# A second buffer for the ternarized weights, and one temporary less, in an attention-plus-FFN kernel

## What is computed

```python
x = x + _layernorm(_L0_attn_ref(_layernorm(x), ...))
x = x + _layernorm(_L0_ffn_ref(_layernorm(x), w1, w2))

# attn: u = x @ W_in.T + b_in;  h = lam * h + gamma * u  (scan over the rows);
#       out = h @ W_out.T + b_out + x
def _quant_weight(w):
    s = jnp.clip(jnp.mean(jnp.abs(w)), EPS, None)
    return jnp.clip(jnp.round(w / s), -1.0, 1.0) * s
# ffn: h = gelu(quant_act(x) @ quant_weight(w1).T); quant_act(h) @ quant_weight(w2).T
# w1: 4096 x 1024, w2: 1024 x 4096
```

## Time and profile before

| | us |
|---|---|
| median of two runs | 4675.93 (4628.41 and 4723.45) |
| profiled execution | 4625.51 |
| its span, slowest core (6) | 4624.0 |
| spans of the eight cores | 4595.0 to 4624.0 |
| busy, core 6: PE / DVE / ACT | 2797.7 / 2941.2 / 1673.8 |
| phase A, from the first x block to B1 | about 70 to 1642 |

### The profile page before, as it was taken

The page is one execution under the profiler, slowest core; times in us unless marked ns, Lnnn a source line. Parts: engine busy times, 40 slices in busy tenths (PEclk is TensorE's granted clock), DMA queues, the critical chain, the costliest instruction groups (busy, mean ns, idle before and its releaser), DMA issues.

```text
span 4624.0 us, 40391 instructions; the slowest of 8 cores (4595.0 to 4624.0 us)
## 1 busy us (share of the span) xinstructions
PE 2797.7 (61%) x11916; PEld 1553.3 (34%) x12080; DVE 2941.2 (64%) x2628; ACT 1673.8 (36%) x2053; POOL 201.5 (4%) x372
## 2 busy tenths in 40 slices
PE   5556554444466635455544554455545279999998
PEld 4445443333355512222222222222222134444444
DVE  4767765566677748788877887788878512222232
ACT  1333322222244435555555455545555211111111
POOL 0000000000000000000000000000000000000000
PEclk8766766666677767777777777777777689999999
DMA  3332344455521131212122112211221366666665
GB/s 128 116 103 100 119 128 134 106 130 139 146 73 55 46 109 55 64 62 62 52 64 64 62 50 64 64 62 51 63 64 62 104 121 155 152 151 154 151 154 128
DMA packets 537185, 447.33 MB, mean 97 GB/s; under 512 B 473206, under 2 KB 473208, under 8 KB 524424
## 3 DMA queue, kind: packets, MB, share of 16 engines
q1 hardware_dynamic: 479624, 184.58, 18.0%
q0 software_dynamic: 57344, 260.15, 16.8%
HBM read 193.02 MB, written 151.00 MB: 74 GB/s over the span
## 4 chain that ended last, share of the span: by engine, by line
PE 41%; DVE 13%; DMA 5%; another core or an unknown queue 2%; issue 2%; ACT 1%; DVEq 0%; ACTq 0%; SPq 0%; POOL 0%; POOLq 0%
PE ps_h L911 22%; PE ps_f L1023 19%; DVE amh L148 6%; DMA qdT<-qd 4%; DVE bd L148 3%; DVE cd L148 2%; DVE qd L148 2%; ACT h_b L148 1%; DMA r2B<-r2scr 1%; DVE irc L148 0%; DVEq L135 0%; DVE sch_all L148 0%; DVE bn L148 0%; DVEq L832 0%
## 5 line engine op out<-in xcount | busy, mean ns | idle before, releaser
L911 PE MATMUL ps_h<-w1T,qdT 128*128 128x512 bf16 x4014 | 1025.6, 419 | 982.8 <-DMA qdT<-qd 976.8
L911 PEld LDWEIGHTS ps_h<-w1T,qdT 128*128 128x128 bf16 x4096 | 429.0, 106 | 1579.4 <-issue 1191.7
L1023 PE MATMUL ps_f<-w2T,qhT 128*128 128x512 bf16 x4014 | 881.3, 379 | 95.0 <-DMA qhT<-qhscr 90.6
L148 ACT ACTIVATE h_b<-ps_h,zerov,g3s 128x512 f32<-128x512 f32 x512 | 397.9, 777 | 569.6 <-PE ps_h L911 569.6
L1023 PEld LDWEIGHTS ps_f<-w2T,qhT 128*128 128x128 bf16 x4096 | 401.1, 98 | 575.3 <-issue 93.2
L735 PE MATMUL ps_u<-lnT,winT 128*128 128x256 f32 x2048 | 390.3, 371 | 226.4 <-ACT gu L148 187.8
L148 DVE BATCH_NORM_STATS2 bn<-ffn 128x6 f32<-128x512 f32 x128 | 88.9, 694 | 596.8 <-ACT ffn L148 590.2
L735 PEld LDWEIGHTS ps_u<-lnT,winT 128*128 128x128 f32 x2048 | 376.5, 281 | 246.2 <-issue 243.5
L148 DVE TENSOR_TENSOR bh<-y0h,r16h 128x4096 bf16<-128x4096 f32 x64 | 283.2, 4425 | 209.4 <-ACT r16h L148 209.4
L148 ACT ACTIVATE y0h<-h_b,halfv,sch_all 128x4096 f32<-128x4096 f32 x64 | 243.2, 3801 | 358.4 <-DVE sch_all L148 358.4
L723 PE MATMUL ps_t<-identt,ln1f 128*128 128x128 f32 x512 | 113.6, 395 | 424.8 <-ACT ln1f L148 299.7
(11 more groups left out here) (99 smaller groups left out, 2408.2 us busy)
## 6 DMA issues: line engine op xcount, KB each, us to landing
qstg<-w SPq DMA_DIRECT2D x64, 1024.0 KB, 5.7
qhscr<-qh_b POOLq DMA_DIRECT2D x64, 1024.0 KB, 5.1
x_buf<-x POOLq DMA_DIRECT2D x32, 1024.0 KB, 6.5
r2scr<-r2b POOLq DMA_DIRECT2D x64, 512.0 KB, 2.9
r2B<-r2scr POOLq DMA_DIRECT2D x64, 512.0 KB, 5.8
r2C<-r2scr POOLq DMA_DIRECT2D x64, 512.0 KB, 5.7
y<-outb POOLq DMA_DIRECT2D x64, 512.0 KB, 3.4
w1tscr<-wtp SPq DMA_DIRECT2D x32, 256.0 KB, 2.7
```

Source lines behind the costliest of these rows:

```text
L148: ins = f(*a, **k)
L911: last = t.matmul(ps_h[q % 6][:], qdTv[ta % 2][:, j, :], w1v[:, j, 512 * hs:512 * (hs + 1)], start=(j == 0), stop=(j == DT - 1))
L1023: last = t.matmul(pslice, qhTv[ta % 2][:, j, :], w2v[:, j, 512 * half:512 * (half + 1)], start=(j == 0), stop=(j == HT - 1))
```

## The change

`t2b` becomes two buffers, used in turn; ternarization c2 waits for the pieces of c2-2 instead of c2-1; SP reads the buffer of c2. `tmp1` is removed, and its place is taken by `t2buf` of the same tile, which is no longer needed once `r2b` is made. ACT's wait ahead of `t2buf` goes from `s_r2v` to the semaphore `s_rs2`, which the maximum now raises. Loads, pieces, their order on SP and the division into slots stay.

```diff
-            tmp1 = sbA("tmp1", [128, D], F32)
             qstg = [sbA(f"qstg{i}", [128, 2048], F32) for i in range(2)]
             t1b = sbA("t1b", [128, 2048], BF16)
-            t2b = sbA("t2b", [128, 2048], BF16)
+            t2b = [sbA(f"t2b{i}", [128, 2048], BF16) for i in range(2)]
@@ tern
-                            if c2 >= 1:
+                            if c2 >= 2:
                                 v.wait_ge(sem("s0_xb"),
-                                          16 * pieces_through(c2 - 1))
+                                          16 * pieces_through(c2 - 2))
                             it = v.scalar_tensor_tensor(
-                                t2b[:], qstg[q % 2][:], nthrv[w][:], t1b[:],
-                                op0=ALU.is_le, op1=ALU.subtract)
+                                t2b[c2 % 2][:], qstg[q % 2][:], nthrv[w][:],
+                                t1b[:], op0=ALU.is_le, op1=ALU.subtract)
@@ r2p
-                        v.tensor_scalar(tmp1[:], r2b[ta % 2][:], bn2r[ta % 2][:, 0:1],
+                        v.tensor_scalar(t2buf[ta % 2][:], r2b[ta % 2][:],
+                                        bn2r[ta % 2][:, 0:1],
                                         None, op0=ALU.subtract)
-                        v.tensor_reduce(am3s[:, ta:ta + 1], tmp1[:], axis=AX.X,
-                                        op=ALU.max, apply_absolute_value=True)
+                        iam = v.tensor_reduce(am3s[:, ta:ta + 1], t2buf[ta % 2][:],
+                                              axis=AX.X,
+                                              op=ALU.max, apply_absolute_value=True)
+                        inc("s_rs2", iam)
@@ ln2p (ACT)
                         if ta >= 2:
-                            a.wait_ge(sem("s_r2v"), ta - 1)
+                            a.wait_ge(sem("s_rs2"), ta - 1)
@@ emit_pieces (SP)
-                            xin = t2b[:]
+                            xin = t2b[c2 % 2][:]
-                            xin = t2b[:, 1024 * j:1024 * (j + 1)]
+                            xin = t2b[c2 % 2][:, 1024 * j:1024 * (j + 1)]
```

## The result

| | before | after |
|---|---|---|
| median of all runs, us | 4641.9 (10 runs) | 4504.6 (13 runs) |
| ratio, 95% interval | | 0.9721 (0.9695 to 0.9747) |
| profiled execution, us | 4625.5 | 4493.8 |
| span of the slowest core | 4624.0 (core 6) | 4492.3 (core 3) |
| mean span of the eight cores | 4608.7 | 4482.5 |

The kernel is 2.8% faster. I had said 4504 us, 2.6%. The medians contain executions in which one die ran at a lower clock; the ratio is made without them.

What follows compares the result with a forecast made beforehand. DVE was taken to set phase A's pace, with the `t2b` waits (172.3 us, 21 times) on its path. The terms were 121.55 us and zeros: 4625.5 - 121.6 = 4503.9 us, range 4480 to 4550.

Steps and rivals of the forecast that it cites:

- (a) The buffers: Slots of blocks 12 to 22: each full slot loses one start-to-start time of `t2b`, 121.55 us over eleven windows.
- The third ternarization's load: Slots' third `qstg` load: hidden ahead of the transposes by 3.3 us (w1) or 0.8 us (w2); taken as nothing, bound 37 us.
- (b) SP: SP's queue: later sets still finish before the next slot, even with slot 14's partial sums (48 to 54 against 55); cost nothing.
- threshold of 17 us a set: SP's queue: with three sets a block and the new 51 us period, SP sets the pace from 17 us a set.
- (c) PE's cover: Second matmul section, 10 us: the shorter slot (16.5 us w1, 15 us w2) still covers it; cost nothing, bound 11 us.
- The price of a missing cover: Blocks without a slot: 37.5 us instead of 34.5; for eleven blocks 33 us.
- (d): DVE's subtraction, written to `t2buf` instead of `tmp1`: stays at 0.75 us, cost nothing; 30 us if it ran at 1.23 us.
- (e): ACT's wait ahead of `t2buf`, moved from `s_r2v` to `s_rs2`: nothing new is awaited and nothing comes earlier; cost nothing.
- PE's clock: Rival, `ln1f` transposes: PE's pause falls from 24.55 to about 12 us, its clock stays up, 20 us gained, 4484 us; chance 0.07.
- Nothing gained: Rival, slots: an unseen wait takes the place of the removed one, 4625 us; chance 0.04.
- slower: Rival, SP's queue: SP becomes the bound beside POOL's transfers; at 24.5 us a set 93 us slower, 4718 us; chance 0.04.
- The sum: Whole kernel: 121.55 us saved and zeros, 4625.5 - 121.6 = 4503.9 us; forecast chance 0.74.

Runs made afterwards that it cites:

- the spread kernels: Changed kernel with its 68 tasks spread over all blocks: two a slot, three every eighth block (ratio 0.9533); or three, then two, then one a slot (0.9508).
- the kernel with two stores: Changed kernel in which SP stores every piece twice and waits for each store; ratio to before 0.9962 (0.9927 to 0.9997), mean span 4589.1 us.
- one wait: Changed kernel in which SP stores each piece once and waits for that store; ratio to before 0.976 (0.9706 to 0.9813), mean span 4506.3 us.

## Why the prediction was right, point by point

**(a) The buffers.** Right, and the whole of it: with only the wait undone the gain is 0.0%. The eleven windows said 121.55 us for core 6; the same windows on all eight cores before have a mean of 125.2 us, and the slots gave up 119.0. `t2b` waits 23.9 us in 10, expected about 22 in 10. One reading in it is wrong: slot 16 had not one wait ahead of `t2b` before but two, 13.59 and 9.31 us. The pieces of slot 15's last chunk go out only behind the thresholds, which slot 16 itself computes:

```profile
919.05 2.35 DVE L148 SCALAR_TENSOR_TENSOR t2b<-qstg,nthrv,t1b 128x2048 bf16<-128x2048 f32 x1 [13.59 <-DMA wtp<-t2b]
```

So one of them stays after (3.48 us on core 3). The sum is not touched by this, as what it took for slot 16, 13.05 us from one `t2b` to the next, is the right window.

The missing 6.2 us (125.2 less 119.0) can be placed slot by slot, as the mean length after less the mean length before, less the window: 0.4 us in slot 12, 1.1 and 1.2 in 13 and 14, 2.8 in 15, 0.2 in 16, and nothing in the slots of w2. In w2's slots, where I had seen only 0.8 us between load and transposes, the forecast held to a tenth.

**The third ternarization's load.** I took nothing for it, and the timeline of slot 13 confirms that the load is not what ends last. But it lands later than before, by the median of all loads 6.3 us instead of 5.7. For the load that the third one waits for, in slots 12 to 15, the means of the cores went from 5.4 or 5.5 us to 5.9 to 6.9 us, and the second transpose landed 10.7 to 12.9 us after the load's issue instead of 10.2 or 10.3. So w1's slots take 17 to 18 us and not 16.5. The mechanism was right; the size of one set of w1 was off by about 1 us. The wait of the third `t1b`, forecast as 2 to 3 us, was 2.2 to 3.6 us in the mean of the cores, but 6.7 us in slot 16, beyond the 4 us named as a sign that the load bounds the slot. It doesn't bound it there: `t2b` waits for the transposes behind it all the same. The median:

```profile
DMA to landing us min/median/max: 4.7/6.3/12.9
```

**(b) SP.** Right for all slots but 15, and there in part: it took 16.6 to 24.4 us on the eight cores, 19.6 in the mean. The prediction had SP ready 48 to 54 us after slot 14's start, against a first need at 55. On core 4 the sums were sent and read back so late that the first load went out 5.7 us into the slot instead of 3.8: from the write of the partial sums to their read SP took 17.6 us there, and 12.3 us in the mean of the cores, where the prediction had taken the 11.4 us of core 6. On the other seven it went out on time, but on four of them the transposes behind it took longer. SP's queue on core 0 (21.5 us):

```profile
787.32 0.26 SPq L657 DMA_DIRECT2D qrow<-scrq  x1
789.13 0.39 SPq L679 DMA_DIRECT2D qstg<-w  x1
...
797.36 1.32 SPq L622 DMA_TRANSPOSE wtp<-t2b  x1
804.21 0.51 SPq L632 DMA_DIRECT2D w1tscr<-wtp  x1
```

The second one took until 804.2, 6.9 us where 3.0 is usual, with nothing else of this core on the DMA engines. Why is open; slot 15 costs 2.8 us in the mean. The threshold of 17 us a set that the prediction gave for the rival held: at a mean of 17.8 us slots 12 to 14 grew by about 1 us, at 23.1 us slots 13 and 14 by 16. What the threshold missed is the block with the partial sums, whose room was smaller, and the third set, which stretches more than a lone one.

**(c) PE's cover.** Right: stretches of 381.5 us against 379.6. PE is done with the second product at 706.4, well inside the slot, and its pause is 13.7 us where it was 24.55. Even the products that ran at a mean grant of 0.57 (16.0 us) were covered: behind the slots of blocks 12 to 21 none made DVE wait, neither before (10 of 80) nor after (5 of 80). One of the usual kind:

```profile
704.31 2.12 PE L704 MATMUL ps_a<-woutT,ybf 128*128 128x512 f32 x8
720.11 1.94 PE L725 MATMUL ps_t<-identt,ln1f 128*128 128x128 f32 x8 [13.68 <-ACT ln1f L148]
```

The price of a missing cover, 3.0 us a block, is confirmed by the spread kernels, where blocks 25 to 31 went from 37.5 us to 34.5 us in the mean behind slots of 7.7 us, and to 34.8 us behind slots of mostly 3.85 us.

**(d) and (e).** Right: 0.75 us, and with the `t2buf` edit alone the stretches of blocks 12 to 22 took 380.8 us in the mean of the cores, against 379.7.

**PE's clock.** This rival fell. After the shorter pause the eight transposes of `ln1f` still take 1.94 us, the time at a granted 0.50, and the stretches didn't get shorter. The mean grant of blocks 12 to 22 rose from 0.66 to 0.69 in the mean of the cores. With two levels, 0.5 and 1, that makes 459 us at the low one before (0.34 x 2 x 675) and 341 us after: 118 us less, about what the slots lost. I read this as idle time at the low level that was taken out, while the work runs at the level it had. The Trainium skill ("TensorE: Matmul & The Clock Gate", Part 1) says that the array drops to half rate when it idles; the transposes behind the pause of 13.7 us agree with it.

**Nothing gained, and slower.** Neither came. The Trainium skill ("DMA: Bandwidth & Descriptors", section "Issuing engines are not separate DMA queues") says that DMAs of different issuing engines run on the same 16 DMA engines and interleave. Crowding of this kind has a size now: the third set of w2 took 22.7 us instead of 15.5 in the kernel with two stores. It costs the changed kernel's w2 slots less than 0.1 us each, as it falls into room that exists.

**The sum.** 4503.9 us was expected for an execution like the profiled one, which came out at 4493.8; that the median of all runs is 4504.6 is chance. The sum started from core 6, whose B1 was 19 us longer than the other seven had it, so it was bound to come out high. By the mean spans it reads 4608.7 - 121.6 = 4487.1 us, and 4482.5 was measured: the other cores had more to gain (125.2), the late sets took 6.2 us of it, and stages outside the change happened to be 7 us shorter.

## What to carry to other kernels

When an in-order engine waits in bursts for a serial partner (here DVE for SP's transposes), a second result buffer is worth one partner's turn for each burst, and the start-to-start time of the blocked operation in the trace is that turn, ready to be summed. Before you buy a third buffer, look which wait is next: here the load stood 3 us behind in the slots of w1 and 0.7 us in those of w2. Where side work comes in bursts and part of the blocks have none, spreading it can be worth nearly as much as the buffer (here 1.9% against 2.8%, and the two add up). It costs no memory, and gives the blocks without side work something to cover their matmuls with. How much cover they need depends on the granted clock of the matmuls: look at the slowest of them, not at the mean.

## What the runs showed that I had not expected

- The same 128x1024 transpose with nothing else of its core in flight takes 3.0 us or 6.9 us. Its 2096 packets took 63.2 ns in the mean in the slow case (797.3 to 804.2 on core 0 after) and 17.8 ns in the quick one (745.5 to 748.6, same core). What the other cores did at that time was not looked into.
- In a kernel where SP stores twice, one w2 transpose occupied SP's queue for 9.59 us and landed 15 us after its issue, beside the next block's stores and load, where 5.6 us and 7.7 us are usual. Room on a DMA queue that was counted from the cost of a lone set can be gone where its work meets a neighbour's.
- Sending the 512 bytes of partial sums to DRAM, from the issue of the write to that of the read behind it, holds SP for 7.6 to 12.2 us over the eight cores before (behind slot 14), 9.6 to 17.6 us after and 7.2 to 9.3 us with one wait. Once it no longer fits between two slots it costs more than its own length: slot 15 grew by 14 us, for a DMA of half a kilobyte.
